# A projection or final product moved ahead of the products with V in every step of a software-pipelined attention

## The reference, cut to what matters

```python
# B=4, L=1024, E=128, 16 heads of 64
h = layernorm(x) * (1 + ca) + sa
qkv = h @ W_qkv + b_qkv                       # Q, K, V: [4, 16, 1024, 64]
scores = einsum('bhqd,bhkd->bhqk', Q, K) / 8
attn = softmax(scores, axis=-1)
out = einsum('bhqk,bhkv->bhqv', attn, V)
x = x + ga * (out.reshape(4, 1024, 1024) @ W_fc + b_fc)
h = layernorm(x) * (1 + cb) + sb
x = x + gb * experts(h)                        # top 2 of 4 small experts, then a layernorm
```

## Time and profile before

| what | value |
|---|---|
| runs without a profile | median 1831.11 us of 3 (1827.95 to 1837.15) |
| profiled execution, its own time | 1838.18 us |
| span from its first to its last instruction | 1836.5 us |
| attention, first maxima to last final product | about 55 to 1607 us of the span |
| mean granted TensorE clock | 0.963 of full speed |
| TensorE matmuls | busy 88% of the span |
| GpSimd, VectorE, ScalarE | busy 62%, 64%, 51% |

### The profile page before, as it was taken

The page is one execution under the profiler, slowest core; times in us unless marked ns, Lnnn a source line. Parts: engine busy times, 40 slices in busy tenths (PEclk is TensorE's granted clock), DMA queues, the critical chain, the costliest instruction groups (busy, mean ns, idle before and its releaser), DMA issues. The chain is left out here.

```text
span 1836.5 us, 29420 instructions
## 1 busy us (share of the span) xinstructions
PE 1616.6 (88%) x8907; PEld 857.5 (47%) x8907; DVE 1171.9 (64%) x2591; ACT 928.5 (51%) x1369; POOL 1136.6 (62%) x517
## 2 busy tenths in 40 slices
PE   4699989999999999999999999999999998756996
PEld 3344444444444444444444444444444444244886
DVE  5567656666666666666666666666666665287887
ACT  3354545555545555555555555555555454325874
POOL 3177666776676667666776777667666766520134
PEclk8699999999999999999999999999999999857999
DMA  2001000000000000000000000000000000110010
GB/s 88 16 24 30 30 30 29 29 29 29 25 18 23 27 29 29 29 29 29 29 24 28 29 29 29 29 29 29 29 29 29 29 25 14 40 47 23 30 35 29
DMA packets 60737, 54.40 MB, mean 30 GB/s; under 512 B 23677, under 2 KB 46746, under 8 KB 60698
## 3 DMA queue, kind: packets, MB, share of 16 engines
q1 hardware_dynamic: 60544, 53.90, 9.4%
q10 hardware_dynamic: 154, 0.03, 0.0%
HBM read 31.35 MB, written 2.36 MB: 18 GB/s over the span
## 5 line engine op out<-in xcount | busy, mean ns | idle before, releaser
L526 POOL TENSOR_TENSOR ACC<-ACC,PR 128x1024 f32<-128x1024 f32 x382 | 913.2, 2391 | 276.2 <-ACT PR L590 259.2
L633 DVE TENSOR_REDUCE NMH<-ps_mx 128x1 f32<-128x512 f32 x1024 | 657.6, 684 | 174.9 <-PE ps_mx L810 174.5
L590 ACT ACTIVATE PR<-ps_s 128x1024 f32<-128x1024 f32 x512 | 497.1, 1023 | 323.3 <-PE ps_s L834 320.9
L845 PE MATMUL ps_o<-PR,V 128*64 128x512 f32 x2048 | 492.7, 602 | 0.0
L810 PE MATMUL ps_mx<-KH,QH 64*128 64x512 f32 x1024 | 256.8, 496 | 112.9 <-DVE NMH L633 105.2
L526 POOL TENSOR_TENSOR ACC<-PR 128x1024 f32<-128x1024 f32 x64 | 151.3, 2365 | 206.9 <-ACT PR L590 206.9
L810 PEld LDWEIGHTS ps_mx<-KH,QH 64*128 64x128 f32 x1024 | 97.6, 185 | 321.1 <-DVE NMH L633 181.9
L845 PEld LDWEIGHTS ps_o<-PR,V 128*64 128x64 f32 x2048 | 129.8, 136 | 232.0 <-issue 197.0
L831 PE MATMUL ps_s<-QH,DL 64*128 64x512 f32 x1024 | 204.1, 391 | 0.0
L834 PE MATMUL ps_s<-QL,DH 64*128 64x512 f32 x768 | 152.9, 390 | 0.0
L828 PE MATMUL ps_s<-QH,DH 64*128 64x512 f32 x768 | 152.8, 391 | 0.0
(11 more groups left out here) (195 smaller groups left out, 2032.8 us busy)
## 6 DMA issues: line engine op xcount, KB each, us to landing
hcur<-hT SPq DMA_DIRECT2D x32, 512.0 KB, 3.3
SUM<-recip_rows SPq DMA_DIRECT2D x128, 128.0 KB, 2.9
Wraw<-in_L_attn_W_qkv SPq DMA_DIRECT2D x32, 192.0 KB, 2.9
x<-in_L_attn_X SPq DMA_DIRECT2D x4, 512.0 KB, 5.3
Wfc<-in_L_attn_W_fc SPq DMA_DIRECT2D x32, 64.0 KB, 2.3
R<-SUM SPq DMA_DIRECT2D x128, 2.0 KB, 1.8
hT<-in_L_attn_X SPq DMA_DIRECT2D x4, 512.0 KB, 6.2
out<-e_res SPq DMA_DIRECT2D x7, 256.0 KB, 2.3
```

What stands on the lines that cost most here:

```text
L526: G.tensor_tensor(ACC[:, ch, :, :], a, PR[:, t, :, :], ALU.add).then_inc(added, 1)
L590: A.activation(PR[:, t, :, :], ps_s[:, t % 2, :, :], ACT.Exp, scale=SCALE).then_inc(exp_done, 1)
L633: D.tensor_reduce(NMH[:, ch, h, i, kc:kc + 1], ps_mx[:, h, :], AX, ALU.max, negate=True).then_inc(mx_red, 1)
L845: last = T.matmul(ps_o[half(h), :], V[:, u, t, half(h)], PR[:, t, h, :], start=(t == 0), stop=(t == 7))
```

## The change

Within each step TensorE issues the unit after the second group of maxima and ahead of the products with V; it was the last thing of the step. The sums go into bank 1 of `ps_mx` in place of `ps_w`, behind the products with V of steps 3 and 7 and directly ahead of `rows`; they stood ahead of the products with V of steps 3 and 5. So the maxima that open steps 4 and 0 also wait until ACT has copied the sums. Both final products now belong to the pair before (steps 3 and 7), Q's second chunk moves to step 4 and V's first to step 5; the inversions stand in steps 1 and 5 and the normalisations in steps 2 and 6. VectorE reduces the first group at the start of the step, and does `early_part` of a unit behind the reduction of the second group in the unit's own step. ScalarE copies `KH` at once behind `Kraw`, with a semaphore of its own, and does `early_part` directly behind the exponentials. SP's order of DMAs follows, and the tail is written anew.

```diff
-        LATE = {0: ("k", 1, 0), 1: ("k", 1, 1), 2: ("q", 1, 0), 3: ("q", 1, 1), 4: ("v", 1, 0), 5: ("fc", -1, 1),
-                6: ("v", 1, 1), 7: ("fc", 0, 0)}
-        SUMS = {3: (-1, 1), 5: (0, 0)}
-        RECIP = {4: (-1, 1), 6: (0, 0)}
-        NORM = {5: (-1, 1), 7: (0, 0)}
+        LATE = {0: ("k", 1, 0), 1: ("k", 1, 1), 2: ("q", 1, 0), 3: ("fc", -1, 0), 4: ("q", 1, 1), 5: ("v", 1, 0),
+                6: ("v", 1, 1), 7: ("fc", -1, 1)}
+        RECIP = {1: (-1, 0), 5: (-1, 1)}
+        NORM = {2: (-1, 0), 6: (-1, 1)}
...
+        def sums_at(n, d):
+            if d == 3 and has(n - 1):
+                return n - 1, 1
+            if d == (5 if isinstance(n, int) and n == NP - 1 else 7):
+                return n, 0
+            return None
...
                 if has(n - 1):
+                    compact_sums(n - 1, 0)
+                    spread_recip(n - 1, 0)
                     compact_sums(n - 1, 1)
                     spread_recip(n - 1, 1)
-                compact_sums(n, 0)
-                spread_recip(n, 0)
...
                     A.activation(Kraw[:, q], ps_w[:, :], ACT.Identity, bias=bias[:, u, 1:2]).then_inc(k_raw, 1)
+                    act.wait_ge(k_raw, 2 * m + ch + 1)
+                    A.activation(KH[:, u, q], Kraw[:, q], ACT.Copy).then_inc(k_hi, 1)
...
-                act.wait_ge(k_raw, 2 * m + ch + 1)
-                A.activation(KH[:, u, q], Kraw[:, q], ACT.Copy)
                 act.wait_ge(k_step, 2 * m + ch + 1)
-                A.activation(DH[:, u, ch * 512 + new.start:ch * 512 + 512], ps_w[:, new], ACT.Copy).then_inc(k_hi, 1)
+                A.activation(DH[:, u, ch * 512 + new.start:ch * 512 + 512], ps_w[:, new], ACT.Copy).then_inc(k_dh, 1)
...
-                A.activation(SUM[:, ch, :], ps_w[:, :], ACT.Copy).then_inc(sums_in, 1)
+                A.activation(SUM[:, ch, :], ps_mx[:, 1, :], ACT.Copy).then_inc(sums_in, 1)
...
+                    done = sums_at(n, d - 1) if d else has(n - 1) and (n - 1, 0)
+                    if done:
+                        sums(*done)
+                    x = late_at(n, u, d - 1)
                     if x:
+                        late_part(*x)
                     exponentials(n, 2 * d)
                     exponentials(n, 2 * d + 1)
+                    x = late_at(n, u, d)
+                    if x:
+                        early_part(*x)
                     if d == 4:
                         copy_o(n, 0)
                     if d == 0 and has(n - 1):
                         copy_o(n - 1, 1)
...
-                    if x:
-                        early_part(*x)
+                    if d in RECIP and has(n + RECIP[d][0]):
+                        invert(n + RECIP[d][0], RECIP[d][1])
                     k = 2 * d + 9
                     if has(group(n, u, k)[0]):
                         reduce_max(*group(n, u, k), 16 * n + k)
+                    x = late_at(n, u, d - 1)
                     if x:
                         late_part(*x)
-                    if d in RECIP and has(n + RECIP[d][0]):
-                        invert(n + RECIP[d][0], RECIP[d][1])
+                    if has(group(n, u, k + 1)[0]):
+                        reduce_max(*group(n, u, k + 1), 16 * n + k + 1)
+                    x = late_at(n, u, d)
+                    if x:
+                        early_part(*x)
                     if d in NORM and has(n + NORM[d][0]):
                         normalise(n + NORM[d][0], NORM[d][1])
-                    if has(group(n, u, k + 1)[0]):
-                        reduce_max(*group(n, u, k + 1), 16 * n + k + 1)
...
             def last():
-                early_part("fc", NP - 1, 1, 0)
+                invert(NP - 1, 0)
                 for t in range(LAST_ON_POOL, 8):
...
+                normalise(NP - 1, 0)
                 invert(NP - 1, 1)
+                early_part("fc", NP - 1, 1, 0)
...
-            def sums(m, ch):
+            def sums(m, ch, groups):
                 pe.wait_ge(added, 14 * m + 7 * ch + 7)
+                wait(pe, sums_in, 2 * m + ch)
+                wait(pe, mx_red, 2 * groups)
...
+                    groups = min(16 * n + k + 2, 16 * NP) if isinstance(n, int) else 16 * n + k + 2
                     if has(group(n, u, k)[0]):
                         if d % 4 == 0:
                             pe.wait_ge(neg_rows, 2 * n + d // 4 + 1)
+                            wait(pe, sums_in, 2 * n - 1 + d // 4)
                         maxima(*group(n, u, k), 16 * n + k)
                     scores(n, u, 2 * d)
                     scores(n, u, 2 * d + 1)
                     if has(group(n, u, k + 1)[0]):
                         maxima(*group(n, u, k + 1), 16 * n + k + 1)
-                    if d in SUMS and has(n + SUMS[d][0]):
-                        freed(previous(n, d, True))
-                        sums(n + SUMS[d][0], SUMS[d][1])
+                    x = late_at(n, u, d)
+                    if x:
+                        freed(before(n, u, d))
+                        unit(*x)
                     if d:
                         times_v(n, u, 2 * d - 2)
                         times_v(n, u, 2 * d - 1)
...
+                    if sums_at(n, d):
+                        sums(*sums_at(n, d), groups)
                     if d % 4 == 3 and has(group(n, u, k)[0]):
                         m, _, ch, _, _ = group(n, u, k)
-                        wait(pe, mx_red, 16 * (2 * m + ch + 1) + (2 if has(group(n, u, k + 1)[0]) else 0))
+                        wait(pe, mx_red, 2 * groups)
                         rows(m, ch)
-                    x = late_at(n, d)
-                    if x:
...
-                        unit(x[0], x[1], parity(u, LATE[d][1]), x[2])
```

More of the change, by code:

```diff
@@ L382, in attention_stage @@
         k_proj, q_proj, v_proj = sem("k_proj"), sem("q_proj"), sem("v_proj")
-        rows_t, sums_mm, fc_mm = sem("rows_t"), sem("sums_mm"), sem("fc_mm")
+        rows_t, sums_mm, fc_mm, k_dh = sem("rows_t"), sem("sums_mm"), sem("fc_mm"), sem("k_dh")
         exp_done, k_raw, k_hi, q_hi, v_copied, o_copied, w_hi, sums_in, s_ident = (
@@ L403, in has, with late_at @@
             return not isinstance(n, int) or 0 <= n < NP
-        def late_at(n, d):
+        def late_at(n, u, d):
             if d < 0:
-                return late_at(n - 1, d + 8)
+                return late_at(n - 1, 1 - u, d + 8)
             kind, off, ch = LATE[d]
-            return (kind, n + off, ch) if has(n) and has(n + off) else None
+            return (kind, n + off, parity(u, off), ch) if has(n) and has(n + off) else None
+        def sums_at(n, d):
[4 more added lines that the diff above has]
+            return None
         def parity(u, off):
@@ L492, in last @@
             def last():
+                compact_sums(NP - 1, 0)
+                spread_recip(NP - 1, 0)
                 compact_sums(NP - 1, 1)
@@ L666, in late_part @@
                     return
-                dve.wait_ge(k_hi, 2 * m + ch + 1)
+                dve.wait_ge(k_dh, 2 * m + ch + 1)
                 if ch == 0:
+                    dve.wait_ge(k_hi, 2 * m + 1)
                     D.scalar_tensor_tensor(DL[:, u, 0:256], ps_w[:, 0:256], bias[:, u, 1:2], KH[:, u, 0:256].bitcast(F32),
@@ L782, in unit @@
                     T.matmul(ps_w[:, :], Wfc[:, u, :], O[:, ch, :], start=True, stop=True).then_inc(fc_mm, 1)
-            def sums(m, ch):
+            def sums(m, ch, groups):
                 pe.wait_ge(added, 14 * m + 7 * ch + 7)
+                wait(pe, sums_in, 2 * m + ch)
+                wait(pe, mx_red, 2 * groups)
                 for h in range(2):
-                    last = T.matmul(ps_w[half(h), :], g.ones[:, 0:64], ACC[:, ch, h, :], start=True, stop=True)
+                    last = T.matmul(ps_mx[half(h), 1, :], g.ones[:, 0:64], ACC[:, ch, h, :], start=True, stop=True)
                 last.then_inc(sums_mm, 1)
@@ L796, in freed @@
             def freed(x):
-                kind, m, ch = x
-                pe.wait_ge({"k": k_lo, "q": q_lo, "v": v_copied, "sums": sums_in, "fc": fc_added}[kind], 2 * m + ch + 1)
+                kind, m, _, ch = x
+                pe.wait_ge({"k": k_lo, "q": q_lo, "v": v_copied, "fc": fc_added}[kind], 2 * m + ch + 1)
             def maxima(m, u, ch, i, kc, count):
@@ L850, in first @@
                 unit("k", 0, 0, 0)
-                freed(("k", 0, 0))
+                freed(("k", 0, 0, 0))
                 unit("k", 0, 0, 1)
-                freed(("k", 0, 1))
+                freed(("k", 0, 0, 1))
                 unit("q", 0, 0, 0)
@@ L856, in first @@
                 maxima(*group(0, 0, 1), 1)
-                freed(("q", 0, 0))
+                freed(("q", 0, 0, 0))
                 unit("q", 0, 0, 1)
@@ L860, in first @@
                 maxima(*group(0, 0, 3), 3)
-                freed(("q", 0, 1))
+                freed(("q", 0, 0, 1))
                 unit("v", 0, 0, 0)
@@ L864, in first @@
                 maxima(*group(0, 0, 5), 5)
-                freed(("v", 0, 0))
```

(29 more changed lines are left out.)

6 lines of the change are left out of this document (removed).

## The result

The changed kernel takes 1883.9 us (median of 4 runs, 1879.1 to 1888.5), the kernel before 1833.4 (4 runs): **1.029 times as long, 95% interval 1.026 to 1.032, slower**. I had forecast 1805 and at most 1830. The profiled execution took 1879.1 us.

The account below looks back on a forecast made before the run. TensorE, 88% busy, bounds the kernel, with attention waits for VectorE's reductions. -3.13 + 1.72 + 0.43 + 0.1 + 0.1 = -0.78 us a pair, -24 for 31 pairs, -2 in the tail: 1831.1 to 1805 us, range 1793 to 1830.

Parts of the forecast that it names:

- The five waits: TensorE's five waits a pair for VectorE's reduction of the first group all go: -3.13 us a pair.
- The turn: After `rows` in steps 3 and 7 the gap to the next maxima becomes bare, 1.12 us each: +1.72 us a pair.
- Small term (a): The unit starts later in steps 1 and 2, behind VectorE's `late_part` and copy: +0.43 us a pair together.
- (b): ScalarE's `DH` is ready before VectorE comes to it, with 0.6 us of cover: no cost.
- (d): Sums alone at a step's end and three added semaphore waits on TensorE: +0.1 us a pair, bounds 0 and 0.4.
- (e): ScalarE's copy of the sums runs beside `rows` and `mask_rows`, so the added wait on `sums_in` costs nothing.
- (c): VectorE's `split_w` in step 6 waits for ScalarE, which copies V first: +0.1 us a pair, bounds 0 and 0.7.
- it fits barely: VectorE's normalisation in steps 2 and 6, taken as 0.69 us, ends just by when the next reduction is due.
- Rival 2: Bare gaps at the turns drop TensorE's clock, at least 1.1 us each: 68 us, kernel about 1873 us; chance 0.06.
- Rival 1: The wait moves from maxima to unit through late `DH`, reductions or `split_w`: 1.0 us a pair, about 1831 us; chance 0.15.
- signs of being wrong: Wait for VectorE's reductions over 1 us a pair, granted clock under 1.00 in the loop, or TensorE waiting for `SUM`.

Follow-up runs that it names:

- e1: The changed kernel with W's split moved from step 6 to step 5: 1804.0 us, 0.984 of the kernel before.
- e3: The changed kernel with six more products that nobody reads in TensorE's stall of step 7: 1863.0 us, 1.017 of the kernel before.
- e7: The changed kernel with W's split moved to step 5 and the sums back in `ps_w` behind `rows`: 1750.2 us, 0.955 of the kernel before.
- e5: The changed kernel with W's split ahead of the normalisation in VectorE's step 6: 1889.3 us, 1.031 of the kernel before.
- e6: The kernel before with GpSimd's additions cut to 8 of 512 columns, softmax sums not computed: 1826.6 us, 0.998 of the kernel before.
- e2: The changed kernel with GpSimd's additions cut to 8 of 512 columns, softmax sums not computed: 1795.1 us, 0.980 of the kernel before.

## Why the prediction was wrong, step by step

- **The five waits, -3.13 us.** Right, in all steps but step 7. There the changed kernel needs 3.92 us from first to second group; elsewhere it is 1.88 us, and 2.25 and 2.20 in steps 0 and 4 with their longer scores. In e1, without the split in step 6, step 7 has 1.88 too.
- **The turn, +1.72.** The mechanism was right, and the size for one of the two turns. From `rows` to the next maxima it is 1.11 us in step 3 (my 1.12), but 1.40 in step 7 in most pairs and 1.51 at most, over my upper end of 1.30: 0.3 us a pair more than the sum has.
- **Small term (a), the unit behind `DL`.** Nearly right: from the second group to the unit it is 0.81 us in step 1 and 0.60 in step 2 where 0.43 is free, 0.55 together for my 0.43. (b), `DH`: right, VectorE does not wait for it. (d), (e): no cost to be seen.
- **The step that failed is (c), with the normalisation's "it fits barely".** I gave the split +0.1 us, bounds 0 and 0.7, from one row, and the normalisation 0.69 from another place. Both have two inputs in SBUF, and in their new place GpSimd's additions run with a gap of 0.1 us at most between them. They took 4.38 us together where I had 1.9 (1.23 and 0.69), and the term, put at 0.1, was **2.03 us of stall** (e3 to e1), with 0.71 us of clock behind it. My bounds came from ScalarE's queue alone; I never asked who else held what VectorE needed. With this loss gone, as in e1, the pair is 46.54 us and the kernel 1804.0, where I forecast 46.67 and 1805. That this is so close is in part luck: the turn costs 0.3 more and (a) 0.1 more than in my sum, the waits give about 0.2 more, and (c) and (d) with their 0.2 cost nothing there. The parts outside the loop offset each other too: the pairs ahead of it gained nothing, and the end of the stage gained over 6 us where I had 2.
- **Rival 2, the clock.** The mechanism was real and its place wrong. I put it at the bare gaps, which e1 shows to be harmless, and priced it at 2.2 us a pair; it struck behind the new stall, in most second pairs, for 0.71 us a pair (e3). On these gaps the Trainium skill's "A second HAM failure mode: psum-queue depth-cycling" (TensorE: Matmul & The Clock Gate) did not come true: in e1 and e7 the granted clock is 1.00 through the loop.
- **Rival 1** had a stall in step 7 through `split_w` at 0.7 us, as an upper end and by another cause. The true one was three times that. Its time was also added wrongly: 1805 + 31 is 1836, not 1831.

Two of my own signs of being wrong came up, the wait for the reductions at 2.0 us a pair and a granted clock of 0.98 in the loop.

Sum of the parts for a pair: 46.54 + 2.03 + 0.71 = 49.28, against 47.57 before: +1.71, 48 us in 28 pairs.

**What holds GpSimd and VectorE apart.** Told as these rows show it (in the result, e5 and e6): an operation of VectorE with both inputs in SBUF, issued while a GpSimd addition runs, ends 0.15 us (128 columns) to 0.55 us (512) after that addition; an addition issued while such an operation runs is 0.1 to 0.35 us longer. Where the two start within 0.02 us of each other, as in step 2, the normalisation keeps its 0.68 us and the addition takes 2.9 in place of 2.37. One input is enough for some operations: in pair 1 a `TENSOR_SCALAR` of 128x512 from SBUF to SBUF (L744) took 1.89 us beside an addition, and the same one 0.42 in e2; the two of this kind took 1.02 and 1.22 in the kernel before. The Trainium skill says it outright (SBUF — State Buffer, "SBUF: two separate sides"): the two engines share a pair of ports, which is "an exclusive lock, not a bandwidth split", taken by VectorE's operations with two SBUF inputs too (against a GpSimd operation that reads SBUF), for a whole instruction. The traces agree: 2.48 us and 0.29 for the same instruction. By that rule, as an estimate with the 2.37 us of an addition, the sum would have had up to one whole addition for each of the two operations of step 6, from 4.8 us down to nothing by phase: it should have been the first rival. Measured were 3.2 us (4.38 against 1.17 in e2), of which TensorE felt 2.03.

Left open: why the clock fell in most second pairs and not in each, although the stall is the same 2.03 us in both; and how the 7.2 us of the first pairs divide. The first `BQ` of pair 2 comes at 177.7 us in the changed kernel, at 172.1 in e1 and at 167.8 in e2, so most of the 7.2 us goes with the place of W's split, and all of it when GpSimd's additions are short. The six operations of `gate_rows` in pair 1 collide too, but they took 9.3 us together before and 8.8 after, so their sum is not what grew.

## What to carry to other kernels

A duration taken from the trace belongs to its phase: before moving an instruction, look at the same instruction elsewhere in the trace (here the two `Wlo` of one pair, 1.03 and 0.28 us), and ask what else was in flight each time. VectorE work on SBUF operands, with two inputs above all, should sit where GpSimd is idle, or where VectorE has a whole GpSimd instruction of slack. A hand-over that must be waited for is a place for work that needs nothing from it, such as the sums behind `rows`.

## What the runs showed of the hardware that I had not expected

- `Wlo`, 128x128 with two SBUF inputs, takes 0.28 us alone and 2.48 us behind the start of a GpSimd addition of 128x1024; the reductions from PSUM beside it keep 1.29 us for two.
- 2.03 us without a product on TensorE brought 3.43 us at a granted clock of 0.51 in most second pairs; with 0.47 us left of it (e3) there was no such fall, and six useless products made the kernel 21 us faster.
